# First batch of layer two gathered, mixed, normed and turned inside the experts' pass

## The reference, cut to what matters

```python
affinity = sigmoid(x @ centroids.T)                  # 16 experts, top 2 of affinity + bias
for e in range(16):
    routed = routed + mask[..., e:e + 1] * (silu(x @ wg[e]) * (x @ wu[e]) @ wd[e])
x = x + shared + routed
h = layernorm(x)                                     # layer two, attention of 16 heads
q, k, v = h @ W_Q[i].T, h @ W_K[i].T, h @ W_V[i].T   # one head i
x = x + (softmax(mask(q k.T) / sqrt(128)) v, all heads) @ W_O.T
x = x + down(silu(gate(layernorm(x))) * up(layernorm(x)))   # weights are lut[idx]
```

## Time and profile before

| | |
|---|---|
| median of 3 runs | 2203.79 us (2198.75 to 2204.74) |
| span of the profiled execution | 2190.4 us |
| median less that span | 13.4 us |
| mean granted TensorE clock over the span | 0.994 |
| TensorE busy | 2123.2 us (97%) |
| VectorE busy | 1694.3 us (77%) |
| ScalarE busy | 1273.8 us (58%) |
| GpSimd busy | 559.2 us (26%) |

### The profile page before, as it was taken

One profiled execution on the slowest core, in us unless ns is written; L12 is line 12 of the kernel. 1 busy time (PEld: TensorE's weight loads), 2 busy tenths in 40 slices (PEclk: granted clock), 3 DMA queues, 4 the chain that ended last, 5 costly groups with the idle time before them and its releaser, 6 DMA issues. The chain is left out here.

```text
span 2190.4 us, 37661 instructions
## 1 busy us (share of the span) xinstructions
PE 2123.2 (97%) x13038; PEld 1854.3 (85%) x13038; DVE 1694.3 (77%) x4387; ACT 1273.8 (58%) x3487; POOL 559.2 (26%) x604
## 2 busy tenths in 40 slices
PE   6899999979999999999999999999999999999997
PEld 5677777758788999899989989998998999899887
DVE  7998886887767887777876877787687778767775
ACT  5644443226637676666665666666566666656662
POOL 0214333430015323122222312222232222222220
PEclk9999999999999999999999999999999999999999
DMA  9001010436522112112111211211121121111100
GB/s 300 1 1 58 20 46 26 170 121 205 172 68 64 59 51 76 39 52 70 54 40 55 82 39 54 69 54 39 57 80 39 54 68 54 39 58 50 39 20 20
DMA packets 88556, 145.81 MB, mean 67 GB/s; under 512 B 8369, under 2 KB 55857, under 8 KB 88369
## 3 DMA queue, kind: packets, MB, share of 16 engines
q1 hardware_dynamic: 67904, 112.73, 16.1%
q0 software_dynamic: 6144, 16.79, 2.2%
q10 hardware_dynamic: 14320, 13.90, 1.9%
HBM read 105.63 MB, written 37.75 MB: 65 GB/s over the span
## 5 line engine op out<-in xcount | busy, mean ns | idle before, releaser
L1018 ACT ACTIVATE pr<-bank,negmax 128x128 f32<-128x128 f32 (+3 forms) x512 | 263.5, 527 | 196.6 <-DVE negmax L1599 196.6
L653 POOL TENSOR_TENSOR wo_low<-wraw_o,wo_high 128x256 fp32r<-128x256 f32 x128 | 94.5, 738 | 1105.0 <-ACT wo_high L705 1105.0
L1136 DVE TENSOR_TENSOR p_low<-bank,p_high 128x512 fp32r<-128x512 f32 (+2 forms) x384 | 190.2, 551 | 100.6 <-ACT p_high L705 100.0
L705 ACT ACTIVATE p_high<-bank 128x512 fp32r<-128x512 f32 (+2 forms) x384 | 177.4, 497 | 149.9 <-PE bank L2121 149.9
L1599 DVE CUSTOM_DVE_ANT_0 bank<-bank,causal 128x128 f32<-128x128 f32 (+3 forms) x512 | 234.7, 520 | 1.1 <-PE bank L1762 1.1
L1626 DVE SCALAR_TENSOR_TENSOR xs<-bank,rinv,xs 128x256 f32<-128x256 f32 x512 | 211.7, 474 | 1.2 <-PE bank L1762 1.2
L1760 PE MATMUL bank<-h_high,wqk_high 128*128 128x512 f32 x512 | 202.6, 396 | 0.0
L1761 PE MATMUL bank<-h_low,wqk_high 128*128 128x512 f32 x512 | 202.5, 396 | 0.0
L1762 PE MATMUL bank<-h_high,wqk_low 128*128 128x512 f32 x512 | 202.3, 395 | 0.0
L1136 DVE TENSOR_TENSOR z_low<-bank,z_high 128x512 fp32r<-128x512 f32 x128 | 88.4, 691 | 130.8 <-ACT z_high L705 130.3
L643 POOL TENSOR_TENSOR wqk_low<-wraw,wqk_high 128x512 fp32r<-128x512 f32 x128 | 165.6, 1294 | 77.3 <-ACT wqk_high L705 77.3
(11 more groups left out here) (338 smaller groups left out, 6327.3 us busy)
## 6 DMA issues: line engine op xcount, KB each, us to landing
wraw<-in_wpair SPq DMA_DIRECT2D x64, 512.0 KB, 4.0
wraw<-in_wpair SPq DMA_DIRECT2D x64, 256.0 KB, 4.4
wraw_o<-in_wpair SPq DMA_DIRECT2D x64, 256.0 KB, 2.5
tokens_by_expert<-zero SPq DMA_DIRECT2D x10, 1024.0 KB, 11.2
xt<-tokens_by_expert SPq DMA_DIRECT2D x40, 256.0 KB, 3.3
expert_results<-ey ACTq DMA_DIRECT2D x40, 256.0 KB, 3.7
wres<-in_wexp SPq DMA_DIRECT2D x1, 6144.0 KB, 20.7
xs<-x_between_stages SPq DMA_DIRECT2D x8, 512.0 KB, 4.5
```

Of the source, the lines that this page charges most:

```text
L653: pool.tensor_tensor(wo2[e][1][:], wraw_o[r][:, e, :], wo2[e][0][:].bitcast(F32), ALU.subtract).then_inc(s_wo, 1)
L705: sc.activation(dst, src, ACT.Copy, scale=scale).then_inc(done, 1)
L1018: ins = sc.activation(pr[:, i, 0:(i + 1) * P], score(i), ACT.Exp, scale=-1.0, bias=negmax[:, i:i + 1], accum_out=rsum[:, i:i + 1])
L1136: v.tensor_tensor(at(parts[1]), src, high_, ALU.subtract).then_inc(done, 1)
```

## The change

1. The gather of batch 0 waits for the stores of the first 32 tiles only (`first_tiles_stored`), and stands ahead of GpSimd's weight operations. It is told to read the first 32 tiles of the table only.
2. VectorE mixes, takes statistics, runs the norm's chain and applies it in portions behind the products of tiles 40 to 56 (`first_batch`); the split into high and low comes at step 63.
3. TensorE turns the normed batch in step 62, into banks 4 and 5 instead of 6 and 7. To free these, `tile_turn_back` writes into the second half of banks 0 and 1, where `tile_turn` also writes, and so it waits as well for ScalarE's copy `xT` of the tile that was turned last (`s_ex2`).
4. All 220 fillers behind the pass, and the waits of TensorE and VectorE for the last store, are gone. ScalarE and SyncE still wait for it, ScalarE now just ahead of the first head's softmax, and GpSimd ahead of the second head's weights.
5. All 82 entries of the unpacking are inside the pass. Batch 0 of x is loaded at pair 12 of the tiles instead of pair 24.
6. `yg` and `h2[0]` are placed outside the space of `wres`.

```diff
-CLOCK_TURNS = (70, 40, 50, 14, 8, 200)
+CLOCK_TURNS = (70, 40, 50, 14, 8)
-NORM_TURNS = 20
-LATE_ENTRIES = 5
+LATE_ENTRIES = 0
+FIRST_TILES = 32
+FIRST_MIX = 40
+FIRST_STATS = FIRST_MIX + 8
+FIRST_CHAIN = FIRST_STATS + 4
+FIRST_APPLY = FIRST_CHAIN + 4
+FIRST_TURN = FIRST_APPLY + 6
+FIRST_SPLIT = FIRST_TURN + 1
+FIRST_BANK = 4
...
+        def first_tiles_stored(engine):
+            for i in range(4):
+                engine.wait_ge(s_yst[i], 16 * FIRST_TILES // 8)
...
+            first_tiles_stored(pool)
+            for n in range(2 * NT):
+                gather(0, n)
             low_qk_weights(0, 0, 0)
             low_qk_weights(1, 1, 0)
             low_v_weights(0, 0)
             low_v_weights(1, 1)
             low_out_weights(0, 0, 0)
             stored(pool)
-            for n in range(2 * NT):
-                gather(0, n)
...
+                if t == FIRST_SPLIT:
+                    layer_norm_high(2, 0, h2[0], FIRST_BANK)
...
-            stored(sc)
-            layer_norm_high(2, 0, h2[0], 6)
             high_q(0)
             high_k(0)
             high_v(0, bank[5][:])
             high_v(1, bank[2][:])
+            stored(sc)
...
+            def first_batch(t):
+                n = t - FIRST_MIX
+                if 0 <= n < 2 * NT:
+                    i, c = n % NT, n // NT
+                    if n == 0:
+                        v.wait_ge(s_x1[0], 16)
+                    if c == 0:
+                        v.wait_ge(s_yg[i], 32)
+                    elif i == 0:
+                        v.wait_ge(s_mix, 1)
+                    ins = v.scalar_tensor_tensor(xs[0][:, i, :], yg[:, i, c, :], wts[:, i, c:c + 1], xs[0][:, i, :],
+                                                 ALU.mult, ALU.add)
...
+                n = t - FIRST_STATS
+                if 0 <= n < NT:
...
+                n = t - FIRST_CHAIN
+                if 0 <= n < 4:
+                    norm_chain(2, 0, n)
+                if t == FIRST_APPLY:
+                    norm_apply(2, 0)
+                if t == FIRST_SPLIT:
+                    layer_norm_low(2, 0, h2[0], FIRST_BANK)
...
             for t in range(NTILE):
                 tile_product(t)
                 unpack_to(early + (t + 1) * (LATE_CHUNK * LUTN - LATE_ENTRIES - early) // NTILE)
+                first_batch(t)
...
             def tile_turn_back(t):
                 pe.wait_ge(s_ea, t + 1)
-                pe.transpose(bank[4 + t % 2][:, 0:P], eh[t % 2][:], ident[:]).then_inc(s_eu, 1)
+                pe.wait_ge(s_ex2, min(t + 3, NTILE))
+                pe.transpose(bank[t % 2][:, D:D + P], eh[t % 2][:], ident[:]).then_inc(s_eu, 1)
...
-            clock_turns(CLOCK_TURNS[5])
-            stored(pe)
...
-            turn(2, 0)
-            clock_turns(NORM_TURNS)
...
+                if t == FIRST_TURN:
+                    turn(2, 0, FIRST_BANK)
```

More of the change, by code:

```diff
@@ L215, in two_layer_program @@
         fw2 = split("fw2", [P, FW])
-        h2 = [split(f"h2{i}", [P, KD, T]) for i in range(2)]
+        h2_odd = split("h21", [P, KD, T])
         f2 = split("f2", [P, KD, T])
-        yg = sb("yg", [P, NT, 2, D])
         q2 = split("q2", [P, T])
@@ L222, in two_layer_program @@
         v2 = [split(f"v2{i}", [P, NT, 2, DH]) for i in range(2)]
+        yg = sb("yg", [P, NT, 2, D])
+        h2 = [split("h20", [P, KD, T]), h2_odd]
         pr = sb("pr", [P, NT, T])
@@ L1518, in _ @@
             v.tensor_copy(expert_row[:], bank[7][0:1, 0:NTILE]).then_inc(s_row, 1)
[L1520 to L1531, removed]
             def low_q(g):
@@ L1714, in mix @@
                 ins.then_inc(s_mix, 1)
[L1716 to L1725, removed]
@@ new lines, in tile_product @@
+            def tile_product(t):
+                v.wait_ge(s_es, t + 1)
+                if t >= 2:
+                    v.wait_ge(s_eu, t - 1)
+                v.tensor_tensor(eh[t % 2][:], esg[t % 2][:], bank[2 + t % 2][:, P:2 * P], ALU.mult).then_inc(s_ea, 1)
+            early = sum(EARLY_ENTRIES)
+            unpack_to(early)
+            for t in range(NTILE):
+                tile_product(t)
+                unpack_to(early + (t + 1) * (LATE_CHUNK * LUTN - LATE_ENTRIES - early) // NTILE)
+                first_batch(t)
@@ L1729, in _ @@
+            unpack_to(LATE_CHUNK * LUTN)
             low_q(0)
@@ L2093, in make_v, with turn @@
                 ins.then_inc(s_v, 1)
-            def turn(n, b):
+            def turn(n, b, bank0=6):
                 pe.wait_ge(s_xn[n], b + 1)
@@ L2231, in head @@
                     scores(g + 1)
-            turn(2, 0)
-            clock_turns(NORM_TURNS)
+            experts = []
+            for t in range(NTILE + 3):
+                if t < NTILE:
+                    tile_turn(t)
+                if 0 <= t - 1 < NTILE:
+                    tile_gate_up(t - 1, experts[t - 1])
+                if t < NTILE and t % NVALUES == 0:
+                    experts += nc.values_load_multi_w_load_instructions(
+                        expert_row[0:1, t:t + NVALUES], engines=(mybir.EngineType.PE,), min_val=0, max_val=NEXP - 1,
+                        bass_reorder=False)[1]
+                if 0 <= t - 2 < NTILE:
+                    tile_turn_back(t - 2)
+                if 0 <= t - 3 < NTILE:
+                    tile_down(t - 3, experts[t - 3])
+                if t == FIRST_TURN:
+                    turn(2, 0, FIRST_BANK)
             make_qk(0)
```

20 lines of the change are left out of this document (12 added, 8 removed).

## The result

The changed kernel takes 2207.18 us (median of 20 runs, 2202.79 to 2211.32), the kernel before 2203.38 (20 runs beside them, one of them at 2356.77): ratio 1.002, 95% interval 1.0013 to 1.0028. I had said 2186, faster with chance 0.95.

The account below looks back on a forecast made before the run. TensorE was taken to wait on one chain behind the pass and to set the pace in it. -25.1 + 1.0 + 1.0 + 5.3 + 0.2 + 0.5 = -17.1 us gave 2186 us, range 2180 to 2194.

Parts of the forecast that it names:

- What bounds the kernel: Behind the pass TensorE's real work stands still for 25.14 us on one chain; in the pass TensorE sets the pace.
- what the change removes: Behind the pass: layer two's first product follows the last down product, at the first filler's place; -25.1 us.
- The new wait in the undisturbed tiles: Turn back's wait for `xT` in about 60 tiles: nothing to 0.1 us each, 6 us at most; 0.5 taken.
- every fourth step is about 0.2 longer: TensorE's register loads in the pass: 0.8 us over 17 tiles, subtracted from VectorE's added delay.
- The first rival: The new wait is not hidden: each undisturbed tile 0.1 us longer, 6 us in all, time 2192; chance 0.13.
- My own sign of being wrong: In the profile of the pass: undisturbed tiles of 1.7 us or more would show the new wait.
- What it adds to TensorE: Eight turns in step 62 of the pass: 1.06 us, taken as +1.0.
- What it adds to ScalarE: Two copies, together 1.09 us, ahead of `xT` in step 63, which the turn back now awaits: +1.0 us.
- What it adds to VectorE: Mix, statistics, chain and norm in steps 40 to 56, plus GpSimd delays and one entry: 9.0 us, 5.3 after slack.
- Sum: All terms together: -17.1 us, span 2190.4 to 2173.3, runs' median 2186.7, rounded down to 2186.
- Gathers and clock: Two rivals: gathers come late, 2190, chance 0.07; clock falls behind the pass and stays there, 2216, chance 0.03.

Follow-up runs that it names:

- A: The kernel before with only the new wait added: each turn back waits for ScalarE's copy of the tile turned last; ratio 1.0112, pass 160.36 us.
- G: The kernel before with a wait added to the turn back for the copy of the tile before (t + 2 instead of t + 3); ratio 1.0016, pass 136.57 us.
- I: The kernel before with the new wait, without register loads behind the pass's head and without their address operations; ratio 0.9998, pass 132.22 us.
- C: The changed kernel without the new wait, first batch turned behind the pass, turn backs in banks 4 and 5; ratio 0.9928, pass 138.41 us.
- the second profile: The changed kernel unaltered, run and profiled again; ratio 1.0024 against the kernel before, pass 163.05 us, gap 1.54 us.
- D: The changed kernel without the new wait: turn backs share bank 4 in halves, first batch turned in two halves through bank 5; ratios 0.9929 and 0.9925.
- H: The kernel before with one register load at the pass's head and none later, experts of tiles 0 to 3 reused; ratio 0.9958, pass 127.20 us.
- F: The changed kernel with register loads of two expert numbers in every second step instead of four in every fourth; ratio 1.0051, pass 171.31 us.
- J: D with the first batch's mix from step 48 instead of 40 and half turns in steps 70 and 76; ratios 0.9904 and 0.9915.
- E: The changed kernel with register loads of eight expert numbers in every eighth step instead of four in every fourth; ratio 1.0051, pass 168.47 us.
- L: D with register loads of two expert numbers in every second step; ratio 0.9968, pass 151.00 us.

## Why the prediction was wrong, point by point

- **What bounds the kernel, and "what the change removes", -25.1 us: right.** Measured 26.86 - 1.53 = 25.3. The first product follows the last down product, no buffer or weight is waited for, and the gathered rows are in time.
- **"The new wait in the undisturbed tiles", 0.5 us with bounds of nothing and 6: the step that failed.** The wait alone costs 23 us by times and 26.7 in the pass. From the earlier trace rows I had asked only whether the array would be free later than the weight load. I did not ask what the sequencer does while it is held. Before, the turn back's only wait was for the product, met 0.8 us ahead of the turn back; now it is for `xT`, met 0.2 ahead. All that TensorE's program still has to issue in a step must fit behind that, and in every fourth step the register loads as well, which the bound of 0.1 us for each tile had no row for. I had named them ("every fourth step is about 0.2 longer"), as a thing that hides a delay, where they were already the sign that the lead was used up. The runs show that the cost needs the late release (A against G) and the loads with the address operations (A against I), and the sequencer's records show it taken up by the load until the late turn back, with a TENSOR_LOAD of 1.04 us where it had taken 0.33. The first rival had the place right and a price of 6 us where 23 was due: that is about what the steps without loads lose (7.0 in A's pass), and the 18.2 of the load steps were not in it. My own sign of being wrong, undisturbed tiles of 1.7 us or more, is what the profile shows (1.76).
- **"What it adds to TensorE", +1.0: right in size.** Step 60, with the eight turns, took 2.63 us, against 1.76 in A: 0.9.
- **"What it adds to ScalarE", +1.0: nothing to be seen.** The wait on `xT` at 624.20 is 0.93 us, but it falls on a load step of 2.80, as long as A's (2.83).
- **"What it adds to VectorE", +5.3: fair without the wait, small with it.** C has 4.7, of which 1.9 in steps 41 and 42 beside GpSimd's splits. In the changed kernel steps 36 to 56 took 46.72 us in the second profile and 44.37 in A: 2.4, the stop included. The long load steps hide most of it.
- **Sum.** By the second profile: -25.3 + 26.65 (wait) + 0.9 (turn) + 1.8 (the rest of 163.05 - 160.36) = +4.0, against 3.9 us by the times taken with it (2208.73 against 2204.83). With my other terms and the wait of the runs, -17.1 - 0.5 + 23 = +5.4: the one term makes the wrong sign.
- **Gathers and clock.** The gathers were not late for VectorE. The clock fell only for some 6 us behind the stop of the first profile, in the pass and not behind it. I had no term for that stop (1.6 us over A's steps in one profile of the changed kernel, 4.9 in the other).

## What to carry to other kernels

Before a wait is added to an engine's program, look not only at whether the data is there in time, but at how far ahead of its engine the sequencer runs at that place, and what it has to issue behind the wait: register loads and address work have no busy time in the profile; they show as a step that is a little long, and their own records stand under their source line. Where two users share a buffer, pick the pairing whose wait is met early (here the copy of the tile before, in D) and not the newest one. Where every awaited result is long there and the engine stands, look at the sequencer's records, whatever engine the row names.

## What the runs showed that I had not expected

- Register loads cost the pass of the kernel before 6.5 us (133.71 against 127.20 in H; the steps without a load and not behind one are the same in both), and both stops beside GpSimd's splits (steps 41 and 45, 1.2 us each) were theirs: without loads those steps take 1.63 us. In the kernel before, theirs are the two loads whose TENSOR_LOAD took over 1 us.
- A wait that is met early costs 2.9 us in 80 tiles (G). The Trainium skill ("Perfetto Trace Analysis", section "Tensor Engine Instruction (MATMUL, LD_WEIGHTS)") has the sequencer push a matmul with its wait into a queue and go on. By that alone G and A would differ little; they differ by 20 us. The trace here does not have the added wait on the matmul: it is a record of the sequencer by itself, and that one holds the sequencer. How many waiting instructions the queue holds no run here shows.
- In some executions several engines stop in steps 37 to 41, while the eight gathers run, with nothing awaited that the profile shows. Steps 38 to 41 take 8.8 us in A, and in the changed kernel 13.7 and 10.4, in F 9.5 with 5.9 more in step 37; without the wait they take 8.0 before, and 12.3 and 7.8 in the two profiles of J. No profile without gathers there has more than 8.9. C and both profiles of D have gathers there and no stop; E's 9.8 hold one of its steps at the lower clock, and L's 9.1 two load steps. What stops the engines stays open.
